# First feed-forward of a fused decoder block: bias rows preset in PSUM by ScalarE, a 13-step scale chain, x dequantised on ScalarE

## The reference

```python
def quant_dequant_fp8(x):            # rows of 128-wide chunks
    xr = x.reshape(M, K // 128, 128)
    amax = max(abs(xr), axis=-1, keepdims=True)
    scale = maximum(amax, 1e-4) / 448
    q = (xr / scale).astype(float8_e4m3fn)
    return q.astype(float32) * scale

X = bf16(x); W0d, W1d, Xd = quant_dequant_fp8(W0), quant_dequant_fp8(W1), quant_dequant_fp8(X)
D = bf16(gelu(Xd @ W0d.T + b0))      # 2048 x 1792
E = quant_dequant_fp8(D) @ W1d.T + b1
return bf16(E)                       # 2048 x 512
```

## Time and profile before

| what | value |
|---|---|
| median of 3 runs | 1655.38 us (1653.3 to 1661.01) |
| profiled execution, its own time | 1660.53 us |
| span of its instructions | 1658.8 us |
| mean granted TensorE clock | 0.962 |
| TensorE busy | 1517.7 us (91%) |
| VectorE busy | 1272.0 us (77%) |
| ScalarE busy | 789.7 us (48%) |
| GpSimd busy | 289.1 us (17%) |
| phase `ffn0` in the span | from 1011.5 to about 1370 us |

### The profile page before, as it was taken

How to read it: one execution, slowest core, us unless ns; L and a number is a source line. 1 busy time by engine, 2 the same in 40 slices (tenths; PEclk the granted TensorE clock), 3 DMA queues, 4 the chain that set the end, 5 groups by cost and what they waited for, 6 DMA issues and landing times. The chain is left out here.

```text
span 1658.8 us, 30014 instructions
## 1 busy us (share of the span) xinstructions
PE 1517.7 (91%) x11398; PEld 807.7 (49%) x11398; DVE 1272.0 (77%) x2386; ACT 789.7 (48%) x1677; POOL 289.1 (17%) x249
## 2 busy tenths in 40 slices
PE   5799999999999999999999987799999987777695
PEld 4355555555555555555555543344555444444253
DVE  6577668677666767777676787899999985999777
ACT  3433434324243343334343233666777754888552
POOL 2001002011011011011020001011111103889520
PEclk7899999999999999999999988899999999899798
DMA  7031321312323231322312212122322240766402
GB/s 266 1 79 50 73 81 26 103 52 52 90 55 61 65 64 52 77 51 65 89 26 65 102 26 90 27 42 45 55 55 44 58 95 4 147 111 110 77 1 102
DMA packets 273838, 113.48 MB, mean 68 GB/s; under 512 B 239154, under 2 KB 255539, under 8 KB 273460
## 3 DMA queue, kind: packets, MB, share of 16 engines
q1 hardware_dynamic: 234820, 78.67, 22.5%
q10 hardware_dynamic: 38896, 33.03, 6.2%
HBM read 44.57 MB, written 11.53 MB: 34 GB/s over the span
## 5 line engine op out<-in xcount | busy, mean ns | idle before, releaser
L585 PE MATMUL pj<-XT,WQ 128*128 128x512 f16 x1536 | 338.8, 381 | 6.4 <-PEq L379 6.4
L627 PE MATMUL xp<-WO,OT 128*128 128x512 f16 x1536 | 340.8, 382 | 4.2 <-DVE X L824 4.2
L627 PEld LDWEIGHTS xp<-WO,OT 128*128 128x128 f16 x1536 | 148.3, 98 | 187.7 <-issue 16.9
L585 PEld LDWEIGHTS pj<-XT,WQ 128*128 128x128 f16 x1536 | 148.6, 98 | 182.0 <-DVE WKV L294 6.7
L824 DVE SCALAR_TENSOR_TENSOR X<-xp,X 128x512 f32<-128x512 f32 x128 | 88.1, 689 | 111.6 <-PE xp L627 110.5
L565 POOL TENSOR_TENSOR VW<-VW,XB 128x1024 f32<-128x1024 f32 x14 | 32.9, 2353 | 758.3 <-DVE VW L107 758.3
L709 ACT ACTIVATE E<-E 128x512 f32<-128x512 f32 x64 | 40.1, 627 | 262.1 <-DVE E L801 262.1
L1028 PE MATMUL db<-W0T,XD 128*128 128x448 f16 x768 | 160.2, 359 | 0.0
L1045 PE MATMUL eb<-W1T,DT 128*128 128x512 f16 x672 | 149.3, 382 | 0.8 <-DMA DT<-HL 0.8
L766 DVE SCALAR_TENSOR_TENSOR QT<-pj,QT 128x512 f16<-128x512 f32 x128 | 87.9, 687 | 55.0 <-ACT QT L688 54.7
L688 ACT ACTIVATE QT<-pj 128x512 f16<-128x512 f32 x128 | 75.6, 590 | 83.5 <-PE pj L585 83.3
(11 more groups left out here) (238 smaller groups left out, 2444.8 us busy)
## 6 DMA issues: line engine op xcount, KB each, us to landing
W0T<-in_L_xattn_wq ACTq DMA_DIRECT2D x7, 1024.0 KB, 5.2
W0T<-in_L_xattn_wo ACTq DMA_DIRECT2D x7, 1024.0 KB, 5.0
CS<-in_ctx SPq DMA_DIRECT2D x4, 1024.0 KB, 10.3
X<-in_x SPq DMA_DIRECT2D x4, 1024.0 KB, 11.2
out<-X SPq DMA_DIRECT2D x8, 512.0 KB, 3.6
XB<-in_L_ffn_W ACTq DMA_DIRECT2D x28, 128.0 KB, 2.7
w0t<-XB ACTq DMA_DIRECT2D x7, 512.0 KB, 3.4
w1t<-W0T ACTq DMA_DIRECT2D x7, 512.0 KB, 3.8
```

The source lines that it names most:

```text
L585: last = pe.matmul(bank[:, :], w, src[:, b, k, tokens], start=n == 0, stop=n == 3 * KC - 1)
L627: last = pe.matmul(xp[i % 2][:, :], OT[:, a, j, i * P:(i + 1) * P], WO[:, b, j, :], start=n == 0, stop=n == 3 * REP - 1)
```

## The change

Three edits are made together, all in `ffn0` or in the scale chain that it shares with the preparation of weights and x.

1. The bias rows are loaded to all 128 partitions. ScalarE writes 64 times the row into the bank with a Copy (`preset_d`, `preset_e`), and all matmuls of the product add to it. The five bias matmuls of a tile go, and so do the three cleared tensors and `scale_biases`. Before the first tile TensorE writes each bank once (`open_banks`). ScalarE presets banks 0 to 2 behind their gelus and bank 3 behind `high_x`, and `eb` behind `out_e`.
2. `quant_scales` has 13 steps in place of 15: the split of `first` into a top and a rest (two instructions) goes, and the two remainders are formed with -512 and with 64 in place of twice -448.
3. `dequantise_x` moves from GpSimd (one instruction) to ScalarE (four instructions, a chunk each), between `d_times_scale(i-1, 0)` and the gelu of bank 3.

```diff
-        lambda: ts(u(top), u(first), 0xFFFFF000, None, ALU.bitwise_and),
-        lambda: tt(rest, first, top, ALU.subtract),
-        lambda: stt(rem, top, -FP8_MAX, clamped, ALU.mult, ALU.add),
-        lambda: stt(rem, rest, -FP8_MAX, rem, ALU.mult, ALU.add),
+        lambda: stt(rem, first, -512.0, clamped, ALU.mult, ALU.add),
+        lambda: stt(rem, first, 512.0 - FP8_MAX, rem, ALU.mult, ALU.add),
...
-            sp.dma_start(B0[:, :], b0.partition_broadcast(1)).then_inc(S["b_ld"], 16)
-            sp.dma_start(B1[:, :], b1.partition_broadcast(1)).then_inc(S["b_ld"], 16)
+            sp.dma_start(B0[:, :], b0.partition_broadcast(P)).then_inc(S["b_ld"], 16)
+            sp.dma_start(B1[:, :], b1.partition_broadcast(P)).then_inc(S["b_ld"], 16)
...
+            def open_banks():
+                for q in range(4):
+                    pe.matmul(db[q][:, 0:NQ], W0T[:, 0, 0, 0:P], W0T[:, 0, 0, 0:NQ], start=True, stop=True).then_inc(S["opened"], 1)
+                pe.matmul(eb[:, :], W0T[:, 0, 0, 0:P], W0T[:, 0, 0, 0:DIM], start=True, stop=True).then_inc(S["opened"], 1)
...
-                    if live(ahead(i, -1)):
-                        pe.wait_ge(S["gelu_done"], count(i, 4, q - 3))
-                    pe.matmul(db[q][:, 0:NQ], ones[:, :], B0S[:, q * NQ:(q + 1) * NQ], start=True, stop=False)
+                    pe.wait_ge(S["bias_set"], count(i, 4, q + 1))
...
-                if live(ahead(i, -1)):
-                    pe.wait_ge(S["eb_done"], count(i, 1, 0))
-                pe.matmul(eb[:, :], ones[:, :], B1S[:, :], start=True, stop=False)
+                pe.wait_ge(S["e_bias_set"], count(i, 1, 1))
...
+            def dequantise_x(i):
+                if live(ahead(i, -1)):
+                    act.wait_ge(S["xt_done"], count(i, 1, 0))
+                act.wait_ge(S["xq_done"], count(i, 1, 1))
+                for k in range(KC):
+                    last = act.activation(QX[:, k, :], VX[:, k, :], ACT.Copy, scale=xs[:, nr(i), k:k + 1])
+                last.then_inc(S["xqs_done"], 1)
...
+            def preset_d(qs):
+                for q in qs:
+                    act.activation(db[q][:, 0:NQ], B0[:, q * NQ:(q + 1) * NQ], ACT.Copy, scale=WEIGHT_SCALE).then_inc(S["bias_set"], 1)
+
+            def preset_after_gelu(i, qs):
+                act.wait_ge(S["gelu_done"], count(i, 4, qs[-1] + 1))
+                preset_d(qs)
+
+            def preset_e():
+                act.activation(eb[:, :], B1[:, :], ACT.Copy, scale=WEIGHT_SCALE).then_inc(S["e_bias_set"], 1)
...
                 act.activation(EB[:, i[1] % 2, :], eb[:, :], ACT.Copy, scale=UNSCALE).then_inc(S["eb_done"], 1)
+                if live(ahead(i, 1)):
+                    act.wait_ge(S["eb_done"], count(i, 1, 1))
+                    preset_e()
...
                 if fixed(i) == -1:
+                    act.wait_ge(S["b_ld"], 32)
+                    act.wait_ge(S["opened"], 5)
+                    preset_d(range(4))
+                    preset_e()
                     high_x(nxt)
...
+                if live(nxt) and live(i):
+                    preset_after_gelu(i, (0, 1, 2))
                 if live(hidden):
                     d_times_scale(hidden, 0)
+                if live(after):
+                    dequantise_x(after)
                 if live(i):
                     gelu(i, (3,))
                 if live(nxt) and fixed(i) != -1:
                     high_x(nxt)
+                if live(nxt) and live(i):
+                    preset_after_gelu(i, (3,))
```

More of the change, by code:

```diff
@@ L45 @@
 PASSES = ((0, 0), (0, 1), (1, 0))
-SCALE_STEPS = 15
+SCALE_STEPS = 13
 SUBNORMAL = 1.5 * 2.0 ** -6
@@ L909, in group @@
                             if i > 0:
-                                scale_weights(g, ((0, 3), (3, 11), (11, SCALE_STEPS))[i - 1])
+                                scale_weights(g, ((0, 2), (2, 9), (9, SCALE_STEPS))[i - 1])
                         for p in prepared(t, last):
@@ L936, in ffn0 @@
         SKV1, WKV1, KT1, V1, project_kv1, high_kv1, low_kv1 = kv1
-        B0, B1, B0S = SH[0:1, 0:INNER], SH[0:1, INNER:INNER + DIM], SH[:, INNER + DIM:2 * INNER + DIM]
-        B1S = sb(ph, "B1S", [P, DIM], BF16)
-        ones = sb(ph, "ones0", [P, P], BF16)
+        B0, B1 = SH[:, 0:INNER], SH[:, INNER:INNER + DIM]
         VX, MX, QX = x_buffers
@@ L954, in ffn0 @@
         names = ("w1_ld b_ld kvw_hi kvw_lo qw_hi "
-                 "xt_done xt_hi xt_lo d_done ones_done bias_zeroed bias_ready gelu_done da_done dstep dw_done dcut dbits dm_done dsum "
+                 "xt_done xt_hi xt_lo d_done opened bias_set e_bias_set gelu_done da_done dstep dw_done dcut dbits dm_done dsum "
                  "dq_done dqs_done dh_done dl_done dt_done e_done eb_done x_done")
@@ L1023, in first_product @@
                         pe.wait_ge(S["xt_lo"], count(i, 1, 1))
-                    if live(ahead(i, -1)):
-                        pe.wait_ge(S["gelu_done"], count(i, 4, q - 3))
-                    pe.matmul(db[q][:, 0:NQ], ones[:, :], B0S[:, q * NQ:(q + 1) * NQ], start=True, stop=False)
+                    pe.wait_ge(S["bias_set"], count(i, 4, q + 1))
                     for n, (k, (a, b)) in enumerate([(k, ab) for ab in PASSES for k in range(KC)]):
                         last = pe.matmul(db[q][:, 0:NQ], XD[:, i[1] % 2, a, k, :], W0T[:, b, k, q * NQ:(q + 1) * NQ],
-                                         start=False, stop=n == 3 * KC - 1)
+                                         start=False, stop=n == 3 * KC - 1, skip_group_check=True)
                     last.then_inc(S["d_done"], 1)
@@ L1045, in second_product @@
                         last = pe.matmul(eb[:, :], DT[:, a, c, :], W1T[:, b, c, :],
-                                         start=False, stop=c == IC - 1 and (a, b) == PASSES[-1])
+                                         start=False, stop=c == IC - 1 and (a, b) == PASSES[-1], skip_group_check=True)
                 last.then_inc(S["e_done"], 1)
@@ L1056, in step @@
                 old, nxt = ahead(i, -2), ahead(i, 1)
-                if fixed(i) == 0:
+                if fixed(i) == -1:
                     pe.wait_ge(w0_ld, 16)
-                    pe.wait_ge(S["ones_done"], 2)
-                    pe.wait_ge(S["bias_ready"], 2)
+                    open_banks()
                 if live(i):
@@ L1164, in step @@
                     act.wait_ge(loaded1["sq_ld"], 16)
+                    act.wait_ge(S["bias_set"], 4 * TILES)
+                    act.wait_ge(S["e_bias_set"], TILES)
                     for j in range(REP):
@@ L1220, in low_keys_values @@
                     low_kv1(dve, db[unit], unit // 2, unit % 2)
[L1222 to L1226, removed]
             def step(i):
@@ L1231, in step @@
                     low_x(nxt)
-                    scale_biases()
                 if live(hidden):
@@ L1272, in _ @@
         def _(pool):
[L1273 to L1278, removed]
             def add_x(i):
@@ L1284, in step @@
             def step(i):
-                older, after = (ahead(i, by) for by in (-3, 2))
-                if live(after):
-                    dequantise_x(after)
+                older = ahead(i, -3)
                 if live(older):
                     add_x(older)
[L1291 to L1295, removed]
             steps(pool, step)
```

## The result

The changed kernel takes 1680.46 us (median of 5 runs, 1678.26 to 1682.25), the kernel before 1660.06 beside it (5 runs, 1653.3 to 1661.65). The ratio is 1.0131, 95% interval 1.0107 to 1.0154: slower by 20.4 us. The forecast was 1680 us: 24.4 more than 1655.4, the median of the first three runs of the kernel before.

What follows compares the result with a forecast made beforehand. It took the ring of VectorE and ScalarE, tied with TensorE, to decide the change: start +4.2, steps 1 to 5 +5.05, steps 5 to 13 +14.2, the last +0.9, sum +24.4 on 1655.4: 1680 us, range 1665 to 1692.

Steps and rivals of the forecast that it cites:

- Two loops: In `ffn0`, TensorE's work (19.55 us a step) beside VectorE and ScalarE (19.48); TensorE's saving worth at most 0.08 alone.
- The x product delays gelu 3: ScalarE's four x products (1.18 us) precede bank 3's gelu, so VectorE's second L1184 starts 1.07 us later each step.
- Two operations: Two steps fewer in VectorE's scale chain, -0.42 us; in step 8 ScalarE reaches L1093 after the chain is done.
- the ring: VectorE and ScalarE waiting for each other in `ffn0`: 19.48 us a step before, 21.26 forecast with the change.
- The 0.85: GpSimd contention on VectorE's second L1202, about 0.85 us; booked at 0 because VectorE then waits for the gelu.
- L1282 at its new place: GpSimd's add starts earlier and holds up VectorE's L102: +0.87 us a step, bounds 0 and 1.16.
- Preset of bank 3: ScalarE's write into PSUM between L1124 and L1108: 0.43 us, bounds 0.29 and 0.84.
- TensorE idles 2.7 us and its clock stays: TensorE's work falls to 18.6 us a step, leaving 2.7 us idle; granted clock stays 1.00, the 2.4 GHz level.
- Start: Start of the phase: ScalarE waits for bias rows on 128 partitions, then presets; first product at 1019.1, total effect +4.2 us.
- the last steps: Steps 13 to 16, including the last tile's second product waiting for a preset: together +0.9 us.
- steps 1 to 5: Steps with a piece of preparation on VectorE, which covers part of the lateness: together +5.05 us.
- The faster rival: Ring relieved to 18.2 us, TensorE's 18.6 the bound: about -8 us, 1647 us total; chance 0.03.

Runs made afterwards that it cites:

- chain of 15: Changed kernel with the scale chain of 15 operations again: 1685.77 us, ratio 1.016 to the kernel before.
- all four edits: Changed kernel: x product last in ScalarE's step, GpSimd's add after both L1202, bank 3's gelu and preset earlier, conversions before bias-row wait at start; 1640.3 us, ratio 0.9906.
- the run where the add waits: Changed kernel with GpSimd's add starting only when both of VectorE's L1202 of the step are done: 1668.13 us, ratio 1.0063.

## Why the prediction was right, point by point

- **Two loops, TensorE's gain worth nothing.** Shown: without its bias matmuls the kernel before keeps its 19.48.
- **The x product delays gelu 3 by 1.18 and so L1184 by 1.07.** Measured 1.17 and 1.05. Shown by moving it alone (-1.19 a step).
- **Two operations are worth 0.42 on VectorE and 0.13 of it in the ring of the steady steps**, since ScalarE arrives later there. Shown by the chain of 15.
- **The 0.85 that GpSimd's product had cost L1202 is booked at 0.** The pair reads 2.08 after, and the time became part of the wait for the gelu.
- **L1282 at its new place: +0.87.** The mechanism was right, the size 0.98 (moving the add alone gives 21.425 - 20.442). L100 takes 1.62, not the 1.50 of the earlier trace rows.
- **Preset of bank 3: 0.43.** Measured 0.46 (1231.71 to 1232.17). The estimate from the Trainium skill's page "ScalarE: Activation LUTs", section "What ACT_TABLE_LOAD costs", was 0.47, and the trace agrees. Together with L1282 this makes most of 21.43 for 21.26, +1.4 us over eight steps.
- **TensorE idles 2.7 us and its clock stays.** The idle time was right, the clock was not: three of the eight steady products ran at a granted clock of 0.84 and took 10.93 us for 9.25. The slack of 2.67 us covered it, so it cost no step anything.
- **Start: +4.2.** Measured +5.13, from two errors of opposite sign. The rows land 5.6 us into the phase for 4.0. Against that, the first product with its bias matmuls took 12.41 us before, at a granted clock of 0.79, and takes 10.56 now, at 0.86: 1.85 less, where the sum had 1.1 for the four matmuls and nothing for the clock.
- **Not in the sum: the chain is shared.** The preparation of weights and x in attention 0 runs `quant_scales` too. Five profiled executions with 15 operations reach the phase at 1011.0 to 1012.3, eight with 13 at 1009.1 to 1010.4, means 1.6 us apart. The chain of 15 in the changed kernel is one of the five, at 1011.16, and nothing else is undone in it: that speaks for the chain, by one execution, where the kernel before alone spreads over 1.3 us.
- **Not in the sum: the layers behind the phase**, 5.6 us, as told.

The sum was 24.4 for the phase, which measured 27.1; the ring's size accounts for 1.4, the start for 0.9, the last steps for 0.3, steps 1 to 5 for 0.15. The total came closer to it than its parts deserve on account of the last two points: 27.1 less 1.7 and 5.6 is 19.9. That 1680.46 lies so near to 1680 is luck in part: the forecast was 2.7 us too low in the phase, had nothing for the 7.2 us outside it, and stood on a base of 1655.4 where the five runs had a median of 1660.06.

The faster rival had its condition named: gelu 3 must not hold L1184. The kernel with all four edits meets it, and there the kernel does get faster, with TensorE busy all the time, as the rival named it. The Trainium skill's page "SBUF — State Buffer", section "Who interferes with whom", was right in its rule on the reduction (it is not held up: L1214 keeps 1.08 beside the add). What speaks for the change there was taken back by ScalarE's order. The prediction tells that rule for VectorE instructions with two inputs and then has it make L1282 dear; but the instruction that the add holds up, L100 (L102 before), reads one tensor. That it is held up shows in its 1.62 us for 0.63, and goes with the add in the run where the add waits.

## What to carry to other kernels

In a ring of engines that wait for each other by hand-written order, an engine at 48% busy over the whole span can still be the wrong place for work. In the phase itself ScalarE was busy 112 of 156 us before the change (steps 5 to 13), and even there the load was not what cost: what counts is which instruction stands behind the new ones, and who waits for it. Four x products of 0.29 us cost 1.2 us a step in front of a gelu and nothing at the end of the same engine's step. When an instruction is taken off a queue, look at what moves up: GpSimd's add lost the instruction that had kept it beside a harmless reduction. And before a busy engine is relieved, measure the pace of each loop separately; 19.55 against 19.48 us is a tie.

## What the runs showed of the hardware that was not expected

- The same program has two lengths behind the phase, 282.7 and 288.5 us, with granted clocks of 0.88 and 0.78 in the same 70 us. Over all thirteen profiled executions the length goes with that clock: 0.78 with 288.5, 0.83 with 284.4 to 284.5, 0.88 with 281.7 to 284.0. The totals of the kernel before fall into two groups as well: in all comparisons they lie between 1651.9 and 1656.1 or between 1658.6 and 1661.7, none between.
- In the changed kernel TensorE's granted clock fell to 0.50 for about 3 us near the start of three of the eight steady products, behind idle times of 2.67 to 2.81 us. Three others had 2.66 to 2.68 us of idle time in front and kept 9.25 us; the last two had 1.0 us. In the kernel before, with TensorE busy 153.5 of 155.8 us, the clock was 1.00 over the same steps. What decides was not found.
- An earlier start of TensorE's first product was paid back in part by a lower granted clock (0.76 for 0.86 in the window of that product): 3.0 us earlier at its start, 1.6 at the first L1104.
- A 128 KB load queued behind one of 448 KB and ahead of one of 3.6 MB took 5.2 us to land.
